# CIN kernel on one core: the rows of finished layers leave on ScalarE's own DMA queue in the first passes, and x of chunk 3 is queued in front of b of chunk 2

## What is computed

```
def _cin(x0, conv_params, split_flags):
    B, _, D = x0.shape
    x = x0
    results = []
    for (W, b), split in zip(conv_params, split_flags):
        h = x.shape[1]
        z = jnp.einsum('bhd,bmd->bhmd', x, x0).reshape(B, h * x0.shape[1], D)
        xk = jax.nn.relu(jnp.einsum('oc,bcd->bod', W, z) + b[None, :, None])
        if split:
            half = xk.shape[1] // 2
            x, xk = (xk[:, :half], xk[:, half:])
        else:
            x = xk
        results.append(xk)
    return jnp.sum(jnp.concatenate(results, axis=1), axis=2)
pooled = _cin(sparse_embed, [(W1, b1), (W2, b2), (W3, b3)], [True, True, False])
return pooled @ Wo.T + bo
```

## Time and profile before

| | before |
|---|---|
| median of 3 runs | 459.78 us (459.44 to 460.38) |
| the profiled execution | 459.7 us, its span 457.9 us |
| granted clock of PE, mean | 0.996 of full speed |
| busy: PE, DVE, POOL, ACT | 449.4, 419.7, 394.2, 309.7 us |
| chain that ended last | PE 84%, POOL 5%, DMA 4% |
| moved by DMA | 75.68 MB, mean 165 GB/s |

### The profile page before, as it was taken

How to read it: one execution, slowest core, us unless ns; L and a number is a source line. 1 busy time by engine, 2 the same in 40 slices (tenths; PEclk the granted TensorE clock), 3 DMA queues, 4 the chain that set the end, 5 groups by cost and what they waited for, 6 DMA issues and landing times.

```text
span 457.9 us, 6067 instructions
## 1 busy us (share of the span) xinstructions
PE 449.4 (98%) x1626; PEld 302.6 (66%) x1626; DVE 419.7 (92%) x486; ACT 309.7 (68%) x391; POOL 394.2 (86%) x145
## 2 busy tenths in 40 slices
PE   8997999999999999999999999999999999999997
PEld 4543565667677776767767677776767767677774
DVE  3975969999999999999999999999999999999997
ACT  5561648868687685868768586775858778586661
POOL 0260678999999898998989899898989999899995
PEclk9998999999999999999999999999999999999999
DMA  7999999998959689495977949597794954722100
GB/s 262 234 224 228 211 213 190 213 223 189 234 106 229 137 185 227 104 224 125 228 145 173 234 103 228 118 221 160 163 226 108 237 110 97 162 46 48 34 12 2
DMA packets 22945, 75.68 MB, mean 165 GB/s; under 512 B 5779, under 2 KB 5907, under 8 KB 18836
## 3 DMA queue, kind: packets, MB, share of 16 engines
q1 hardware_dynamic: 22932, 75.52, 74.7%
HBM read 59.51 MB, written 0.00 MB: 130 GB/s over the span
## 4 chain that ended last, share of the span: by engine, by line
PE 84%; POOL 5%; DMA 4%; SPq 3%; DVE 2%; ACT 1%; issue 1%; DVEq 0%; POOLq 0%
PE y_ps L924 25%; PE y_ps L930 14%; PE y_ps L912 14%; PE y_ps L914 14%; PE y_ps L920 7%; POOL zl L629 5%; DMA shifted<-xt_dram 4%; PE y_ps L936 3%; PE y_ps L890 3%; DVE z L672 2%; SPq L362 1%; SPq L372 1%; PE y_ps L855 1%; PE y_ps L916 1%; PE y_ps L932 1%
## 5 line engine op out<-in xcount | busy, mean ns | idle before, releaser
L629 POOL TENSOR_TENSOR zl<-z,zh 128x1024 fp32r<-128x1024 f32 (+1 forms) x135 | 386.3, 2894 | 37.3 <-ACT zh L534 37.0
L672 DVE TENSOR_TENSOR z<-a_ps,b_fac 128x512 f32<-128x512 f32 (+2 forms) x258 | 273.5, 1085 | 20.9 <-PE y_ps L936 11.7
L534 ACT ACTIVATE zh<-z 128x1024 fp32r<-128x1024 f32 (+1 forms) x135 | 168.7, 1250 | 111.2 <-DVE z L672 110.7
L930 PE MATMUL y_ps<-zl,w_high 128*128 128x512 f32 x315 | 146.8, 558 | 0.3 <-POOL zl L629 0.2
L912 PE MATMUL y_ps<-zh,w_high 128*128 128x512 f32 x315 | 124.8, 396 | 1.3 <-ACT results L494 0.7
L914 PE MATMUL y_ps<-zh,w_low 128*128 128x512 f32 x315 | 123.2, 391 | 0.0
L924 PE MATMUL y_ps<-z,w_raw 128*128 128x512 f32 x240 | 122.3, 590 | 0.0
L930 PEld LDWEIGHTS y_ps<-zl,w_high 128*128 128x128 f32 x315 | 59.0, 188 | 65.2 <-issue 57.7
L912 PEld LDWEIGHTS y_ps<-zh,w_high 128*128 128x128 f32 x315 | 59.1, 188 | 15.5 <-issue 1.5
L914 PEld LDWEIGHTS y_ps<-zh,w_low 128*128 128x128 f32 x315 | 59.2, 188 | 13.5 <-issue 0.5
L924 PEld LDWEIGHTS y_ps<-z,w_raw 128*128 128x128 f32 x240 | 45.1, 188 | 9.9
(11 more groups left out here) (69 smaller groups left out, 212.9 us busy)
## 6 DMA issues: line engine op xcount, KB each, us to landing
b_fac<-xt_dram SPq DMA_DIRECT2D x52, 512.0 KB, 8.6
shifted<-xt_dram SPq DMA_DIRECT2D x60, 256.0 KB, 4.8
a_rep<-x_sb SPq DMA_DIRECT2D x91, 128.0 KB, 2.9
shifted<-xt_dram SPq DMA_DIRECT2D x60, 128.0 KB, 5.1
b_fac<-xt_dram SPq DMA_DIRECT2D x16, 256.0 KB, 10.4
a_rep<-x_sb SPq DMA_DIRECT2D x62, 64.0 KB, 2.5
w_raw<-w_dram SPq DMA_DIRECT2D x2, 640.0 KB, 11.4
shifted<-x_dram SPq DMA_DIRECT2D x2, 512.0 KB, 5.7
```

The lines of the kernel that those rows point to most:

```text
L534: nc.scalar.activation(zh[:, slot, 0:end - native, :], z[:, slot, native:end, :], ACT.Copy).then_inc(zh_ready, 1)
L629: nc.gpsimd.tensor_tensor(zl[:, slot, 0:end - native, :], z[:, slot, native:end, :], zh[:, slot, 0:end - native, :].bitcast(F32), ALU.subtract
L672: return nc.vector.tensor_tensor(dst, factor.unsqueeze(1).to_broadcast(list(dst.shape)), others, ALU.mult)
L930: mm = nc.tensor.matmul(y, wh[layer][:, w, :], zl[:, slot, t, :], start=False, stop=end_here)
```

## The change

There are three edits. The five DMAs of a spread become a function of their own, `spread_rows`, that takes the engine that issues them. In SP's written-out order the two spreads are gone, and `load_x(3)` stands in front of both halves of b of chunk 2, behind a wait for the rows of layer 1 of chunk 1. ACT issues the two spreads instead: that of layer 2 of chunk 0 in pass 1, that of layer 1 of chunk 1 in pass 2, and in pass 2 it moves `a_to_psum(3, 1, 0)` ahead of two `results_to_sbuf`.

```
+        def spread_rows(queue, layer, halves):
+            top = X_HALF[layer].start
+            for k, to, rows, count in ((0, 0, 0, 2), (0, 2, 0, 2), (1, 1, 0, 2), (1, 3, 0, 1), (1, 0, 1, 1)):
+                if k in halves:
+                    queue.dma_start(a_rep[layer + 1][Q * to:Q * (to + count), k, :],
+                                    x_out[layer][top + Q * rows:top + Q * (rows + count), :]
+                                    ).then_inc(a_spread[layer + 1][k], 16)
...
-            def spread(layer, c, halves=(0, 1)):
+            def spread(layer, c):
                 sp.wait_ge(x_ready[layer], c + 1)
...
+                spread_rows(sp, layer, (0, 1))
...
             load_b_half(1, 0)
-            spread(2, 0, (1,))
             load_b_half(1, 1)
-            spread(1, 1)
+            sp.wait_ge(x_ready[1], 2)
+            load_x(3)
             load_b_half(2, 0)
             load_b_half(2, 1)
-            load_x(3)
...
                             x_to_sbuf(2, 0)
                             a_to_psum(3, 0, 0)
+                            act.wait_ge(x_ready[2], 1)
+                            spread_rows(act, 2, (1,))
...
                             x_to_sbuf(1, 1)
+                            act.wait_ge(x_ready[1], 2)
+                            spread_rows(act, 1, (0, 1))
+                        if pos == 6:
+                            a_to_psum(3, 1, 0)
                             results_to_sbuf(2, 0)
                             results_to_sbuf(1, 1)
-                        if pos == 6:
-                            a_to_psum(3, 1, 0)
```

## The result

The change made the kernel slower. The median is 460.71 us over 20 runs (459.15 to 462.45), beside 459.47 us over 20 runs of the kernel before; the ratio is 1.0033, with a 95% interval of 1.0019 to 1.0047. By the ratio that is 1.5 us more (the two medians differ by 1.2), where 1.8 us less were forecast. The profiled execution of the changed kernel took 459.15 us, with a span of 457.4 us and a mean granted clock of 0.996. It is the shortest of the 20, and 17 of them had a mean clock of 0.993 (median 460.8).

What follows compares the result with a forecast made beforehand. PE bounds from the fourth pass; earlier passes are bound by one full DMA queue, losing 6.9 us. With T = 63.4, chunk 4 starts at 65.2 + 26.95 + 1.74 = 93.9, 1.8 us earlier: 459.7 - 1.8 = 457.9 us, range 454.8 to 460.4.

Steps and rivals of the forecast that it cites:

- When do the rows of a3 land?: Chunk 0, layer 3: a3 rows on ACT's queue land at 37 to 38, before PE runs dry at 39.53.
- at worst as now: Upper bound on the landing of a3's rows on ACT's queue: 40.0, the time of the kernel before.
- the 2.50 us and 1.74 us: PE's wait before 42.04 and the low-clock loss in the eight products after it; both were to go, 4.24 us.
- T: Landing of a2 of chunk 2, gating PE's layer 1 of chunk 3; 64.3 before, forecast 63.4, PE idling 3.4 us there.
- The fourth: Rival: a3's spread starves and lands at 40, PE keeps 2.50 and 1.74; sum unchanged, no chance of its own.
- The third: Rival: the two queues disturb each other, so T is late; at 5% less rate T = 66.4 and 460.9 us; chance 0.10.
- ACT's issues: The last five spread issues on ACT, at SP's 0.61 us each, end near 36.5 inside ACT's 5.40 us wait, costing nothing.
- DVE's wait of 3.81: DVE's wait before 64.22 for x of chunk 3; goes, as x lands 10.3 us earlier, near 53.
- the 8192 KB: Bytes the queue moved from 23.24 until a2 of chunk 2 landed at 64.3, in 41.1 us, 204 GB/s.
- the 2.05: Extra time from layer 1 of chunk 3 to layer 1 of chunk 4, 29.00 against 26.95 us; it should go.
- 93.9: Forecast start of PE's layer 1 of chunk 4, 65.2 + 26.95 + 1.74, in place of 95.68.

Runs made afterwards that it cites:

- the wait filled: The changed kernel with five extra unused float32 products on PE before the group that waits for a3; 459.28 us, ratio 0.9989.
- The order of the loads alone: The kernel before with only load_x(3) moved ahead of both halves of b of chunk 2, spreads still on SP's queue; 457.89 us, ratio 0.9964.
- the order of the change: The kernel before, all on SP's queue: b of chunk 1 ahead of both spreads, x of chunk 3 ahead of b of chunk 2; PE waits 6.19 us; 461.93 us.
- the kernel that waited 2.34 us: The changed kernel with only a3's spread back on SP between the halves of b of chunk 1; 457.44 us, ratio 0.9952.

## Why the prediction was wrong

**The step that failed** is the first, "When do the rows of a3 land?": "The x and b in front are many KB and these rows few, so I take 37 to 38". They landed at 40 to 42.3, later than before, and beyond the worst of the two bounds, which was the time of before. The argument took it that rows on another queue pass whatever SP has queued. They passed only a part: some 2 us worth of it (42.35 beside 44.42 on SP's queue with the same loads in front). Their former place on SP's queue, ahead of the second half of b of chunk 1, was worth 4.4. The bound "at worst as now" left out that the edit takes the rows away from that place while b moves up into it, which the order on SP before and after shows. The bound had to be the landing behind all of b of chunk 1.

**The low clock** was misplaced with it. The prediction took the 2.50 us and 1.74 us away and charged 1.74 once at T. In the change there is no wait at T, and the low clock stays behind the wait for a3: 17 of 20 executions have a mean clock of 0.993, where the kernel before lost 0.004 or nothing. The experiment with the wait filled measures it at 2.0 us. That one profiled execution of before stood in for a mix of executions with and without a low clock (40 and 44 of 84) was an error of its own: a 1.74 in the sum was a price that only a part of them pays.

**The rivals.** The fourth named what happened, "the spread is starved on its queue and lands at 40", but it was priced as leaving the sum where it is, since it kept the old wait and no more. It had to be worked out with the rows landing behind b, at which the wait grows, and it is this case that ended on the slower side. The third had the right side for another reason: the queues did not disturb each other, T came earlier and not later, and that its 460.9 is close to the measured time is luck.

**The steps that held.** ACT's issues cost 0.59 to 0.76 us on the average of a group and lie within its wait for a3. x of chunk 3, whose last DMA was issued at 38.3 and took 14.7 us, landed at 53.0, as predicted (near 53), and DVE's wait of 3.81 went to 0.85. T was taken as 63.4 and measured 62.4 (58.36 + 4.0): the 8192 KB moved in 38.6 us from 23.82, 217 GB/s in place of 204. There the prediction set against it what the Trainium skill says in "DMA: Bandwidth & Descriptors", section "Issuing engines are not separate DMA queues", that a second issuer saves only issue time; T measured 1.9 us earlier than before, where that reading had left it. The order of the loads has a part in this: alone, on one queue, it gives T = 63.3, 40.4 us for the same bytes (before: 41.1). The spreads on ACT's queue alone give 38.8 us, but the five of a2 alone, with x in front, no less than the order does (40.4). No wait for a2 of chunk 2 appeared, since PE came late itself. Pass 3 gave back 1.86 of the 2.05. The order of the loads alone gives 1.6 us, close to the 1.8 forecast for the whole change: there PE does hang on T (63.3 against the 63.4 forecast) and starts layer 1 of chunk 3 at 65.04 (65.2). That chunk 4 then begins at 93.82 (93.9) is luck, as pass 3 still takes 28.78 us with the clock at 1.00 behind T, where the forecast had 26.95 and 1.74 for the clock. Beside the late a3 it gives nothing: with x of chunk 3 at its old place the change takes 460.64 us, and with x in front 460.71, since PE reaches the place of x so late that it waits for neither.

**What stays open.** Why no packet of ACT's queue moved for the first six microseconds is not shown; it was only seen that it does not happen when nothing of b is queued. What made the two queues quicker in three traces and not in a fourth, below, is open. Why one execution loses the clock for longer than another with the same waits is not shown either.

## What to carry to other kernels

Before a small urgent transfer is moved to another engine's queue, see what its place in the old queue kept out from in front of it, and bound its landing by everything that will then be queued by the time it is issued. Where two edits are bundled, run each alone: here one gained 1.6 us alone and the other lost 1.1, and together they lost 1.5, for the wait that the one brings covers the one that the other removes. Where a small transfer stands between two engines on the path and the destination can be written by an engine that waits for it anyway, drop the DMA: for a3 and a2 together that was worth 3.6 us more than the better order of the loads alone (0.9964 to 0.9886), where the best order of the queues gained 2.2 us over the kernel before. For a3 alone it brought nothing that can be told, as the next wait took its place.

## What the runs showed of the hardware

- A second queue passed little of what the first had queued by then: the rows took 9.7 to 10.9 us behind b of chunk 1 and 2.5 to 3.0 us with only x of chunk 2 in flight. In the change no packet of the second queue moved for the first six microseconds; from 36 us on the queues moved about as many packets each.
- From 36 to 48 us the DMA engines moved 254, 249 and 242 GB/s in three traces, one execution each, with all eight DMAs of the spreads on ACT's queue (the change, the spreads alone, the wait filled), and 227, 235 and 232 in three with all of them on SP's (before, the order of the loads alone, the order of the change). With five of the eight on ACT's queue it was 227.
- The clock fell with the length of PE's wait, but not the same way in each execution: 0.989 to 0.993 in 11 of 12 executions of the kernel that waited 6.19 us, 0.993 or below in 18 of 20 of the change (4.34 us in its trace), 0.996 or 1.0 in equal parts in the kernel that waited 2.34 us, and 1.0 in 10 of 12 with the wait filled.
